# Two groups of heads side by side over the key chunks, and a feed-forward of eight tiles in one piece

## What is computed

```python
xn   = (x - mean) * rsqrt(var + 1e-5) * gamma + beta
q, k, v = split(xn @ w_qkv.T)            # 16 heads of 16, q * 16 ** -0.5
attn = softmax(causal(q @ k.T)) @ v      # 4096 x 4096 scores a head
x1   = layernorm(x + attn)
h    = silu(x1 @ w1.T * s1) * (x1 @ w2.T * s2)     # 256 -> 1024
h    = gelu(h @ h1.T * h1s)                         # 1024 -> 1024
h    = gelu(h @ h2.T * h2s)                         # 1024 -> 1024
out  = layernorm(x1 + h @ w3.T * s3)                # 1024 -> 256
```

## Time and profile before

| | before |
|---|---|
| median of the runs | 2429.91 us |
| the profiled execution: its time, its span | 2433.38 us, 2431.6 us |
| TensorE matmuls, busy | 2338.7 us (96%) |
| VectorE, busy | 1759.6 us (72%) |
| ScalarE, busy | 1437.3 us (59%) |
| GpSimd, busy | 176.6 us (7%) |
| first score, last copy of ACC | 55.8 us, 1718.8 us |
| granted clock of TensorE, mean | 0.981 of full |

### The profile page before, as it was taken

How to read it: one execution, slowest core, us unless ns; L and a number is a source line. 1 busy time by engine, 2 the same in 40 slices (tenths; PEclk the granted TensorE clock), 3 DMA queues, 4 the chain that set the end, 5 groups by cost and what they waited for, 6 DMA issues and landing times. The chain is left out here.

```text
span 2431.6 us, 40685 instructions
## 1 busy us (share of the span) xinstructions
PE 2338.7 (96%) x15360; PEld 1403.5 (58%) x15360; DVE 1759.6 (72%) x4155; ACT 1437.3 (59%) x2830; POOL 176.6 (7%) x245
## 2 busy tenths in 40 slices
PE   5999999999999999999999999999899999799997
PEld 3544544455445445555544555454588887588886
DVE  6889888888889887888878888895335543444543
ACT  3466666677777777777767777779523332332331
POOL 1110000111000101100010210001000000000000
PEclk7899999999999999999999999999899999899999
DMA  4000001100000200000020100205400000400000
GB/s 130 18 18 18 19 18 32 42 18 19 19 13 7 51 23 19 19 19 18 1 53 19 25 12 19 70 1 191 141 1 9 9 1 9 151 1 9 9 1 18
DMA packets 43289, 77.19 MB, mean 32 GB/s; under 512 B 10448, under 2 KB 20688, under 8 KB 41680
## 3 DMA queue, kind: packets, MB, share of 16 engines
q1 hardware_dynamic: 37344, 54.60, 8.3%
q0 software_dynamic: 5744, 19.92, 2.5%
HBM read 36.73 MB, written 4.19 MB: 17 GB/s over the span
## 5 line engine op out<-in xcount | busy, mean ns | idle before, releaser
L530 ACT ACTIVATE PR<-bank 128x512 f32<-128x512 f32 (+3 forms) x2304 | 1108.6, 569 | 334.1 <-PE bank L773 332.0
L598 DVE TENSOR_REDUCE pm<-bank 128x1 f32<-128x512 f32 x1792 | 1118.0, 683 | 195.0 <-PE bank L748 187.0
L787 PE MATMUL bank<-PR,V 128*17 128x512 f32 (+3 forms) x4608 | 561.1, 564 | 2.0 <-ACT PR L530 1.2
L1125 PE MATMUL bank<-e_hid,e_h_sb 128*128 128x512 f32 x2048 | 478.1, 395 | 0.0
L768 PE MATMUL bank<-MR,ones 64*128 64x512 f32 (+3 forms) x2304 | 455.6, 387 | 2.7 <-ACT MR L521 0.7
L1125 PEld LDWEIGHTS bank<-e_hid,e_h_sb 128*128 128x128 f32 x2048 | 384.8, 188 | 92.0
L952 ACT ACTIVATE e_tmp<-bank,e_s_sb 128x512 f32<-128x512 f32 x128 | 88.3, 690 | 342.5 <-PE bank L1125 341.9
L768 PEld LDWEIGHTS bank<-MR,ones 64*128 64x128 f32 x2304 | 228.2, 185 | 76.8 <-ACT PR L530 32.1
L748 PE MATMUL bank<-KA,QX 64*128 64x512 f32 (+2 forms) x992 | 252.6, 451 | 8.4 <-DVE pm L598 2.2
L1070 DVE CAST e_hid<-e_tmp 128x512 fp32r<-128x512 f32 x128 | 54.5, 426 | 267.7 <-ACT e_tmp L952 267.7
L748 PEld LDWEIGHTS bank<-KA,QX 64*128 64x128 f32 x992 | 125.7, 183 | 207.5 <-DVE pm L598 124.2
(11 more groups left out here) (97 smaller groups left out, 1627.6 us busy)
## 6 DMA issues: line engine op xcount, KB each, us to landing
e_h_sb<-in_h_dram POOLq DMA_DIRECT2D x4, 4096.0 KB, 20.8
xnT<-in_h_dram SPq DMA_DIRECT2D x8, 1024.0 KB, 6.1
KA<-qk_hi SPq DMA_DIRECT2D x96, 64.0 KB, 2.2
KA<-qk_lo SPq DMA_DIRECT2D x96, 64.0 KB, 2.2
QX<-qk_hi SPq DMA_DIRECT2D x80, 64.0 KB, 2.2
QX<-qk_lo SPq DMA_DIRECT2D x80, 64.0 KB, 2.3
xres<-in_x_dram SPq DMA_DIRECT2D x8, 512.0 KB, 7.3
out_dram<-e_y SPq DMA_DIRECT2D x8, 512.0 KB, 2.9
```

The lines of the kernel that those rows point to most:

```text
L530: act.activation(PR[:, s % NPB, h, off:QB], ring_bank("score", s, h)[:, off:QB], ACT.Exp).then_inc(exp_done, 1)
L598: dve.reduce_max(pm[:, B % 2, i, a, p, 2 + c:3 + c], bank[:, :], AX.X).then_inc(mx_done, 1)
L787: last = pe.matmul(ACC[32 * h:32 * h + VW, off:QB], V[:, v_tile(B, t), GH * (B // NJ % 2) + h, :], PR[:, s % NPB, h, off:QB], start=(t == ...
L1125: last = pe.matmul(RING[(4 + n) % NR][:, :], w[:, c, P * o:P * (o + 1)], hid[:, (T + layer) % 2, part, c, :], start=(c == 0 and part == 0) ...
```

## The change

- **Order of blocks.** Groups 0 and 1 go through the chunks side by side, then groups 2 and 3: B % 16 // 2 is the chunk, and the lengths are 4, 4, 8, 8, ... 32, 32 steps, twice. Both share V of a chunk, so a V unit is B // 2.
- **Key slots.** 18 in place of 12 (`NKA` 14, `NKB` 4): the 16 blocks of a pair hold their keys. Blocks 18 and later take slots of the first pair when these are free, which the planner asks for (`free`): units of such a block start no earlier than 6 steps after.
- **Transposed chunks.** `xnT` holds three chunks. The first two are made in the introduction, the others between steps, GpSimd normalising them. Each is stored in the memory of `out` (`keep`) and read back for groups 2 and 3 (`fetch`).
- **Introduction.** Projections of blocks 0 to 3 stand in it; one deviation for chunks 2 to 7 together.
- **Masked maxima.** On the diagonal's chunk one masked maximum over all 128 (i + 1) columns, written into the bank itself, takes the place of the two operations.
- **Test of the weights.** 512 KB at a time, so 22 chunks in place of 11.
- **Feed-forward.** One program of eight tiles, no loop, no clearing. The last tile is normalised and stored in four parts.
- The scratch memory for the DMAs that GpSimd issues is set to 8192 bytes.

```diff
-NK, NKA = 12, 8
+NKA, NKB = 14, 4
+NXT = 3
...
+DEVIATIONS = ((0, 1), (1, 2), (2, NJ))
+INTRO_QK = 4
+STACK_STEPS = 6
+
+def chunk_of(B):
+    return B % PAIR // 2
+
+def group_of(B):
+    return 2 * (B // PAIR) + B % 2
...
-            s = max(s, START[B - NQ + 1] if B >= NQ else 0)
+            s = max(s, self.free[B])
+            if B % 2 == 0 and B < PAIR:
+                for stage, lead in (("scale", 3), ("norm", 1)):
+                    after.setdefault(max(0, s - lead), []).append((stage, B // 2))
...
-        for c in range(NJ):
-            ops.append(("stat", c))
-            if c > 0:
-                ops += [("inverse", c - 1), ("scale", c - 1), ("norm", c - 1)]
-            if c in (1, 5):
-                ops.append(("qk", c // 4))
-        ops += [("inverse", NJ - 1), ("scale", NJ - 1), ("norm", NJ - 1), ("qk", 2), ("v", 0)]
-        ops += [("unit", 0, n) for n in range(len(maxima_of(0)))] + [("rowmax", 0), ("neg", 0), ("maxT", 0)]
+        ops += [("stat", 0), ("inverse", 0), ("scale", 0), ("norm", 0), ("qk", 0), ("qk", 1)]
+        ops += [("stat", 1), ("inverse", 1), ("scale", 1), ("norm", 1), ("v", 0)]
+        ops += [("stat", c) for c in range(2, NJ)] + [("inverse", 2)]
+        ops += [("unit", 0, n) for n in range(len(maxima_of(0)))] + [("rowmax", 0), ("qk", 2), ("neg", 0), ("maxT", 0), ("qk", 3)]
...
+                free = self.free[queue[at][0]]
+                if 0 < free and s < free + STACK_STEPS:
+                    goal = done
+                    break
...
+            def keep(u):
+                sp.wait_ge(xnt_done, EC * (u + 1))
+                sp.dma_start(kept[:, :, QB * u:QB * (u + 1)], xnT[:, u % NXT, :, :]).then_inc(xnt_kept, 16)
+
+            def fetch(u):
+                j = u - NJ
+                sp.wait_ge(xnt_kept, 16 * min(NJ, u - NXT + 1))
+                sp.wait_ge(v_ready, u - NXT + 1)
+                sp.wait_ge(qk_ready, 2 * (u - NXT) + 2)
+                sp.dma_start(xnT[:, u % NXT, :, :], kept[:, :, QB * j:QB * (j + 1)]).then_inc(xnt_load[u % NXT], 16)
...
             for B in range(NB):
                 stack(B)
-                if B % NJ == 0 and 0 < B < NB - NJ:
-                    load_weights(B // NJ + 1)
+                if B % 2 == 1 and B < PAIR:
+                    keep(B // 2)
+                if B in (PAIR - 2, PAIR - 1):
+                    load_weights(B - PAIR + 4)
+                if B % 2 == 0 and NJ <= B // 2 + 1 < NU:
+                    fetch(B // 2 + 1)
...
+            def normalise(c):
+                pool.wait_ge(rstd_done, 3)
+                pool.wait_ge(xnt_ready, EC * c)
+                for i in range(TI):
+                    pool.tensor_scalar(xn[:, i, :], xres[:, TI * c + i, :], mv[:, c, i, 0:1],
+                                       rstd[:, c, i, :], ALU.subtract, ALU.mult).then_inc(xn_done, 1)
...
-                    if i > 0:
-                        dve.reduce_max(pm[:, B % 2, i, a, p, 1:2], bank[:, 0:P * i], AX.X)
-                    dve.tensor_tensor_reduce(out=masked[:, p, a, :], in0=bank[:, P * i:P * (i + 1)], in1=below[:, :],
-                                             scale=1.0, scalar=-3.0e38, op0=ALU.add, op1=ALU.max,
+                    own = bank[:, 0:P * (i + 1)]
+                    dve.tensor_tensor_reduce(out=own, in0=own, in1=below[:, QB - P * (i + 1):QB], scale=1.0,
+                                             scalar=-3.0e38, op0=ALU.add, op1=ALU.max,
                                              accum_out=pm[:, B % 2, i, a, p, 0:1]).then_inc(mx_done, 1)
...
-        NB = 4
+        NB = NJ
...
+                for i in range(TI):
+                    sp.wait_ge(o_done, NB + i)
+                    sp.dma_start(out_v[NB - 1, :, i, :], y[:, i, :]).then_inc(stored, 16)
...
-        with nc.Fori(0, NJ // NB) as b:
-            with ExitStack() as ctx_b:
-                program(b)
-            clear(nc, sems)
+        with ExitStack() as ctx_b:
+            program()
...
-    nc = _bacc.Bacc("TRN2", target_bir_lowering=False, num_devices=1)
+    nc = _bacc.Bacc("TRN2", target_bir_lowering=False, num_devices=1, dynamic_dma_scratch_size=8192)
```

More of the change, by code:

```diff
@@ L22 @@
 VH = 2 * GH
+PAIR = 2 * NJ
 NU = G // 2 * NJ
 LOW_BITS = 12
-WC = 2048
+WC = EC * QB
 EPS = 1e-5
@@ L43, with last_of, k_slots @@
 STACK_AHEAD = 8.0
-INTRO_QK = 3
-def tiles_of(B):
-    return TI * (B % NJ + 1)
+DEVIATIONS = ((0, 1), (1, 2), (2, NJ))
[5 more added lines that the diff above has]
+    return 2 * (B // PAIR) + B % 2
+def tiles_of(B):
+    return TI * (chunk_of(B) + 1)
+def last_of(B):
+    return B - B % PAIR + PAIR - 2 + B % 2
+def k_slots():
+    slots = {PAIR - 3: NKA, PAIR - 1: NKA + 1, PAIR: NKA + 2, 0: NKA + 3}
+    slots.update((B, n) for n, B in enumerate(B for B in range(PAIR + 2) if B not in slots))
+    order = [b for g in range(2) for b in range(g, PAIR, 2)]
+    former = dict(zip(range(PAIR + 2, 2 * PAIR), order))
+    slots.update((B, slots[b]) for B, b in former.items())
+    return [slots[B] for B in range(NB)], former
+K_SLOT, K_FORMER = k_slots()
 START = [sum(tiles_of(b) for b in range(B)) for B in range(NB + 1)]
@@ L55, in offset @@
 def offset(B, t):
[L57 removed]
+    return max(0, P * (t - TI * chunk_of(B)))
 def v_unit(B):
[L62 removed]
+    return B // 2
 def maxima_of(B):
[L67 removed]
+    return [(i, c, p) for i in range(TI) for c in range(chunk_of(B) + 1) for p in range(2)]
 def max_width(B, i, c):
[L71 removed]
+    return QB if c < chunk_of(B) else P * (i + 1)
 class Schedule:
@@ L81, in __init__ @@
         self.ops = []
+        self.free = [max(self.slot_free(b) for b in range(B + 1)) for B in range(NB)]
         self.intro()
@@ L223, in clear, with attend @@
     nc.all_engine_barrier()
-def attend(nc, x, gamma, beta, wqk, wv, xres, ident, eps, KB, QX, banks, ff_weights, low_bits, early):
+def attend(nc, x, gamma, beta, wqk, wv, out, xres, ident, eps, KB, QX, banks, ff_weights, low_bits, early):
     with ExitStack() as ctx:
@@ L263, in attend @@
         low_max = sb("low_max", [P, 1], int32)
-        xn = PR[:, NPB - 1, :, :].rearrange("p h q -> p (h q)").rearrange("p (s i e) -> p s i e", s=2, i=TI)
-        chunks = [xnT[:, 0, WC * slot:WC * (slot + 1)].bitcast(int32) for slot in range(2)]
-        low_row = masked[0:1, 0, 0, :]
-        ored = xnT[:, 1, 0:WC].bitcast(int32)
+        turned_chunk = [xnT[:, n, :, :].rearrange("p f q -> p (f q)") for n in range(NXT)]
+        chunks = [turned_chunk[n].bitcast(int32) for n in range(2)]
+        low_row = below[0:1, 0:P]
+        ored = turned_chunk[2].bitcast(int32)
+        kept = out.rearrange("o (f p t) e -> p f (o t e)", f=EC, p=P)
         ACC = banks[NRING]
@@ L284, in attend @@
         xnt_done = sem("xnt_done")
+        xnt_kept = sem("xnt_kept")
+        xnt_load = [sem(f"xnt_load{n}") for n in range(NXT)]
         qk_ready = sem("qk_ready")
@@ L473, in _ @@
                     split(op[1])
+                if op[0] == "scale" and op[1] > 1:
+                    normalise(op[1])
                 if op[0] == "out":
@@ L548, in _ @@
             for op in PLAN.ops:
-                if op[0] == "stat":
+                if op[0] == "inverse":
                     deviation(op[1])
@@ L667, in _ @@
                     inverse(op[1])
-                if op[0] == "scale":
+                if op[0] == "scale" and op[1] <= 1:
                     normalise(op[1])
@@ L726, in project_v @@
             def project_v(u):
-                pair, j = divmod(u, NJ)
-                if u == 0:
-                    pe.wait_ge(xnt_done, EC)
+                pair = u // NJ
+                if u < NJ:
+                    pe.wait_ge(xnt_done, EC * (u + 1))
+                else:
+                    pe.wait_ge(xnt_load[u % NXT], 16 * len([n for n in range(NJ, u + 1) if n % NXT == u % NXT]))
                 if u == NJ:
@@ L786, in product @@
                 for h in range(GH):
-                    last = pe.matmul(ACC[32 * h:32 * h + VW, off:QB], V[:, v_tile(B, t), GH * (B // NJ % 2) + h, :],
+                    last = pe.matmul(ACC[32 * h:32 * h + VW, off:QB], V[:, v_tile(B, t), GH * (B % 2) + h, :],
                                      PR[:, s % NPB, h, off:QB], start=(t == 0), stop=(t == tiles_of(B) - 1))
@@ L861, in feed_forward_exact @@
         yrstd = sb("y_rstd_sb", [P, TI, 1])
-        h_load = [sem(f"h_load{i}", kept=True) for i in range(2)]
+        h_load = [sem(f"h_load{i}") for i in range(2)]
         s_load = sem("s_load")
@@ L960, in _ @@
                         copy_x1T(T + 1)
-                std_y(NB - 1)
+                for i in range(TI):
+                    std_last(i)
             @block.vector
@@ L965, in tokens @@
                 def tokens(T):
-                    return [xres[:, bass.ds(TI * NB * b + TI * T + i, 1), :].rearrange("p o e -> p (o e)")
-                            for i in range(TI)]
+                    return [xres[:, TI * T + i, :] for i in range(TI)]
                 def x1_statistics(T):
@@ L1079, in _ @@
```

(8 more changed lines are left out.)

163 lines of the change are left out of this document (81 added, 82 removed).

## The result

The changed kernel takes 2413.69 us (median of 4 runs, 2411.32 to 2415.1), the one before 2430.11 beside it: ratio 0.993, interval 0.9913 to 0.9947. It is faster by 16.4 us, and 19.7 slower than forecast. The miss has one place. From the last copy of ACC on, the changed kernel needs 683.3 us where the one before needed 712.8: 29.5 less, forecast 26.5. Up to that copy it needs 1729.6 us where the one before needed 1718.8: 10.8 more, and the forecast was 9.7 less.

A forecast was written before the change was run, and what follows sets the result against it. TensorE bounds the feed-forward; a loop of TensorE, VectorE and PSUM banks bounds attention, VectorE above two units a step. Attention -9.7, loop -23.8, end -2.7: -36.2 from 2433.4 gives 2397.2, less 3.5 to the median, 2394 us; range 2372 to 2416.

The forecast's parts named there:

- the loop and the end: Feed-forward: removing the hole between the loop's rounds saves 23.8 us; less clearing, branching and last store save 2.7.
- masked maxima: Attention, diagonal tiles: fusing two VectorE operations into one saves 9 us, between 0 and 26, or a loss.
- four of 0.3 to 1.3 us are hidden: Attention: GpSimd's normalisation of a chunk, four operations asked for two steps before use, costs no time.
- placing of the units between the pairs: Attention: the order of blocks saves 4 us, the units' placing adds 1.8; later periods make two units a step.
- transposes between steps: Attention: six chunks transposed between steps at 1.4 us each, bound 1.0 to 2.2, add 8.4 us.
- the stall at blocks 8 and 9: Attention: ScalarE's 5.18 us wait between projections in adjacent steps goes with the new order, saving 5.0 us.
- the saving of the order itself: Attention: the new order of blocks thins units above 2.33 a step, saving 4 us, between 0 and 12.
- the fewer units in the cold start: Attention: fewer units of maxima in the cold start save 1.5 us.
- I take the 26: Masked maxima: 26 us of VectorE saved if masked columns cost like reduced ones and bank writes like SBUF; a third counted.
- Rival D: Masked maxima: writing the bank costs VectorE more; at double per column, 167 us of VectorE, about 2520 us; chance 0.05.
- rival B: Attention: chunks between steps hold the queues, 3 to 4.5 us each, six times, 18 to 27: 2415 us; chance 0.12.
- Two steps of lead: Attention: GpSimd's normalisation is asked for two steps, over 5 us, before use; the argument against chunks holding the queues.

The follow-up runs named there:

- experiment 1: The kernel before with only the change's feed-forward of eight tiles, attention untouched: 2402.16 us, ratio 0.9886.
- experiment 2: The changed kernel with the masked maxima of before, a reduction and a masked maximum into SBUF: 2415.72 us, ratio 0.9938.
- experiment 13: The changed kernel with chunk 3's normalisation on GpSimd at step 17 instead of step 22: 2409.36 us, ratio 0.9907.
- experiment 9: The changed kernel with seven query slots instead of six and the ninth V projection 19 steps earlier: 2409.5 us, ratio 0.991.
- experiment 10: The changed kernel with the six chunks between steps transposed twice on TensorE and copied twice on ScalarE: 2424.15 us, ratio 0.9973.
- experiment 5: The kernel before with the change's feed-forward of eight tiles and query/key block 9's projection one step later: 2399.11 us, ratio 0.9867.
- 11: The kernel before with the eight-tile feed-forward, block 9's projection one step later and masked maxima in one operation written to SBUF: 2387.84 us, ratio 0.9822.
- 14: The kernel before with the eight-tile feed-forward, block 9's projection one step later and one-operation masked maxima written into the PSUM bank: 2394.87 us, ratio 0.9847.
- experiment 3: The changed kernel with the fused masked maximum written to SBUF as bfloat16 instead of into the bank: 2409.0 us, ratio 0.9915.
- experiment 8: The changed kernel with query/key block 3's projection moved from the introduction to the first steps: 2409.92 us, ratio 0.9911.

## Why the prediction was right or wrong

Right: the feed-forward. The terms of the loop and the end were 26.5 together; the profile shows 29.5 and experiment 1 gives 28.2. Eight transposes and the last tile went as described. The weights' test stayed hidden: its last operation was over at 1727.7 us, and the reciprocal of block 31's sums started at 1731.6, when ScalarE had delivered them. Its 21 steps took 56.5 us (25.9 busy, 30.6 waiting), where 52 were forecast. The loads, from the page's part 6 (KB each, median us from issue to landing):

```profile
xnT<-in_h_dram SPq DMA_DIRECT2D x16, 512.0 KB, 4.1
```

A straight line through 4.1 us for 512 KB and 6.1 for 1 MB leaves 2.1 us at size zero, an estimate from two sizes, each with two loads in flight. With that the trace agrees with the fixed 2.0 us that the Trainium skill states in "DMA: Bandwidth & Descriptors", section "Anatomy of one DMA — SWDGE (gpsimd) path", though on another queue's path.

Right too: a step with two units at 2.69 to 2.74 (forecast 2.70), block 31 at 66, the first exponential (58.26 us; 1.5 after 57.0 was forecast), and the third of VectorE's time that is on the path.

Wrong: the attention, forecast 9.7 off, measured 11.5 on, 21.2 apart. Its steps:

| step of the prediction | forecast | shown | difference |
|---|---|---|---|
| masked maxima | -9 | -2.0 (experiment 2) | 7.0 |
| "four of 0.3 to 1.3 us are hidden" on GpSimd | 0 | +4.3 (experiment 13) | 4.3 |
| placing of the units between the pairs | in the -4 + 1.8 | +4.2 more (experiment 9) | 4.2 |
| transposes between steps | +8.4 | +8.5 to +10.5 (experiment 10, an estimate by doubling) | 0 to 2.1 |
| the stall at blocks 8 and 9 | -5.0 | at least -3.0 (experiment 5, which removes half of it) | 0 to 2.0 |

The first three are 15.5 of the 21.2, all five at most 19.6. Each difference of medians is good to some 2 us. Two terms no run took alone: the saving of the order itself (-4), and the fewer units in the cold start (-1.5), which no row had shown either. What is missing may lie there.

The step that failed most is the masked maxima: "I take the 26". It joined two conditions, what a masked column costs and what writing into the bank costs. The first held. The second did not, and it took 17 to 19 us of the 24 that the fusion saves. By the page's busy times VectorE loses 23.1 us by the fusion into SBUF (experiment 5 to 11) and 5.9 by the one into the bank (experiment 5 to 14). Written to SBUF the fusion gives 6.7 us in the changed order (experiment 3 against 2) and 11.3 in the order of before, so the 9 would have been a fair price for that form. (24 is from start to start, medians: four tiles with the reduction are 1831 ns in the kernel before, 202 + 336 + 469 and four times 206; fused into SBUF they are 211 + 345 + 478 + 611 = 1645; the difference comes 128 times.) Rival D had the mechanism (writing the bank costs more), priced it by the column, and put its deciding point at 0.10 us an instruction; it is 0.037 by the medians, the same at every width. It was right in kind, and too small to change the sign.

The second is rival B, seen once in six chunks. The prediction had bounded the operation at 1.3 us, so the 4.8 of a chunk lay inside its bounds, but it asked only whether the chunk would be ready, not what stands behind it in GpSimd's queue. "Two steps of lead" were over 5 us for full steps; steps 22 and 23, at a block's end, last 2.25 and 0.85. The mask of step 23 paid. Rival B's time, 2415, is 1.3 from the measured one, and that is luck: it had 18 to 27 us from six chunks, and 4.3 came from one.

The third is where the prediction counted units a step over whole periods ("both make two a step"). Blocks 16 and 17 have 0 and 2 units in eight steps, against 5 and 14 in the first twelve of a period before. Units that don't go there go into fuller steps, at 0.9 us each (11.7 us for 13). Its 67 and 64 units above two a step are totals less two a step too: counted step by step they are 82 and 101, since other steps have fewer than two.

The introduction: the first score came at 51.1 us, not 55, and it gave nothing, since the forecast time of the first exponential came about, and by the path that the prediction named (ScalarE waits for block 2's stack ahead of the first exponential). It did not ask whether the fourth projection had to be there; 3.8 us of the changed kernel are that choice (experiment 8).

## What to carry to other kernels

Price an operation by its destination as well as its inputs, and where a saving depends on two prices that no row shows, put their ends in the range and a value between them in the sum. When work moves to an engine that is mostly idle, look at what is queued behind it there, in the shortest steps and not in the mean one. A buffer count and the order of a DMA queue belong together: with one slot more, units came earlier, met a queue that nothing had waited for, and lost 17 us in one step.

## What the runs showed of the hardware

- VectorE's fused mask and maximum of a PSUM bank costs 37 ns more (by medians, from its start to that of the accumulator's read) when it writes back into that bank than when it writes SBUF, at 128 as at 512 columns. Only operations directly behind another such one show it (249 against 211 ns at 128 columns); the first of a row shows 206 to 217 in both forms. The read of its accumulator shows 140 ns against 83.
- GpSimd takes 1.22 us for (x - mean) * rstd over 128x256 with two values per partition; VectorE takes 0.41 for the same in the introduction.
- One wait of TensorE of 2.44 us was followed by 3 us at a granted clock of 0.50. The transposes there took 1.97 us in place of 1.09.
- Block 0 of the changed kernel and its variants ended between 78.4 and 82.6 us with the same first exponential within 1.1 us; the clock rose earlier or later. A difference of 3 us that is already there at the end of block 0 is no effect of a later edit.
